# Squares of queries and keys summed in halves and stacked beside the rounded inputs: random features in two matmul passes

## The reference, cut to what matters

```
def _apply_kernel(x, orf):                      # orf: 256 x 64
    proj = einsum('bhld,md->bhlm', x, orf) / d_k ** 0.25
    norm = sum(x * x, axis=-1, keepdims=True) / (2.0 * sqrt(d_k))
    return (exp(proj - norm) + EPS) / sqrt(m)
q_phi, k_phi = _apply_kernel(q, orf), _apply_kernel(k, orf)
kv   = einsum('bhlm,bhld->bhmd', k_phi, v);  ksum = sum(k_phi, axis=2)
num  = einsum('bhlm,bhmd->bhld', q_phi, kv); den = einsum('bhlm,bhm->bhl', q_phi, ksum)
out  = num / den[..., None]
```

## Time and profile before

| | |
|---|---|
| median of 3 runs | 1614.45 us (1612.59 to 1615.34) |
| the profiled execution | 1616.33 us |
| its span | 1614.8 us |
| PE busy (matmul) | 1411.8 us, 87% |
| PEld busy | 1245.2 us, 77% |
| DVE busy | 758.5 us, 47% |
| ACT busy | 465.8 us, 29% |
| POOL busy | 383.8 us, 24% |
| PE's granted clock, mean | 0.949 |

### The profile page before, as it was taken

One profiled execution on the slowest core, in us unless ns is written; L12 is line 12 of the kernel. 1 busy time (PEld: TensorE's weight loads), 2 busy tenths in 40 slices (PEclk: granted clock), 3 DMA queues, 4 the chain that ended last, 5 costly groups with the idle time before them and its releaser, 6 DMA issues.

```text
span 1614.8 us, 26325 instructions
## 1 busy us (share of the span) xinstructions
PE 1411.8 (87%) x8396; PEld 1245.2 (77%) x8460; DVE 758.5 (47%) x1492; ACT 465.8 (29%) x777; POOL 383.8 (24%) x380
## 2 busy tenths in 40 slices
PE   5788878967879999999999999997999499999980
PEld 2566666967879999999999999996888488888860
DVE  7754443414334545444444545345454425444536
ACT  7412222401013333333232424243222113223310
POOL 7422343233221010101010101002224211222233
PEclk9999999988889999999999999999999599999995
DMA  4100111334222020202020202003144326665657
GB/s 150 54 32 23 53 59 56 97 115 123 84 71 85 20 90 14 91 13 91 13 91 13 91 13 78 0 1 120 57 144 139 141 74 237 239 238 215 213 199 279
DMA packets 64532, 158.06 MB, mean 98 GB/s; under 512 B 7978, under 2 KB 28922, under 8 KB 64032
## 3 DMA queue, kind: packets, MB, share of 16 engines
q1 hardware_dynamic: 55200, 127.20, 22.4%
q0 software_dynamic: 9280, 30.17, 6.0%
HBM read 119.98 MB, written 55.71 MB: 109 GB/s over the span
## 4 chain that ended last, share of the span: by engine, by line
PE 76%; DMA 7%; DVE 6%; issue 5%; ACT 2%; POOL 2%; DVEq 1%; SPq 1%; POOLq 0%; ACTq 0%
PE PB L1562 7%; PE PB L1564 7%; PE PB L1563 7%; PE PB L1738 5%; PE PB L1739 5%; PE PB L1741 5%; PE PB L1598 4%; PE PB L1621 4%; PE PB L1466 4%; DMA y_scratch<-xrow 3%; PE PB L1507 2%; PE PB L1544 2%; PE PB L1508 2%; PE PB L1509 2%; PE PB L1545 2%
## 5 line engine op out<-in xcount | busy, mean ns | idle before, releaser
L1562 PE MATMUL PB<-xh,hw 128*128 128x416 f32 (+1 forms) x576 | 206.0, 358 | 7.0 <-POOL orfl L758 7.0
L1564 PE MATMUL PB<-xh,hw 128*128 128x416 f32 (+1 forms) x576 | 204.1, 354 | 0.0
L1563 PE MATMUL PB<-xl,hw 128*128 128x416 f32 (+1 forms) x576 | 203.8, 354 | 0.0
L1738 PE MATMUL PB<-mwh,mth 128*128 128x512 f32 x368 | 149.4, 406 | 1.3 <-issue 1.3
L1466 PE MATMUL PB<-ohs,ohd 128*128 x471 | 107.4, 352 | 46.5 <-DVE ohs L1116 31.6
L1739 PE MATMUL PB<-mwl,mth 128*128 128x512 f32 x368 | 144.7, 393 | 0.0
L703 POOL CAST hw<-hraw 128x1024 fp32r<-128x1024 f32 x24 | 25.1, 1047 | 466.6 <-PE PB L1564 465.8
L1466 PEld LDWEIGHTS PB<-ohs,ohd 128*128 x534 | 52.3, 99 | 100.3 <-issue 82.3
L1562 PEld LDWEIGHTS PB<-xh,hw 128*128 128x128 f32 x576 | 109.4, 190 | 8.4 <-POOL orfl L758 7.2
L1741 PE MATMUL PB<-mwh,mtl 128*128 128x512 f32 x368 | 114.4, 392 | 0.0
L1563 PEld LDWEIGHTS PB<-xl,hw 128*128 128x128 f32 x576 | 109.5, 190 | 1.3
(11 more groups left out here) (260 smaller groups left out, 3135.3 us busy)
## 6 DMA issues: line engine op xcount, KB each, us to landing
mraw<-expert_w SPq DMA_DIRECT2D x64, 512.0 KB, 7.4
slot_y<-x SPq DMA_DIRECT2D x7, 2560.0 KB, 12.2
slot_y<-ybuf SPq DMA_DIRECT2D x46, 256.0 KB, 3.3
count_rests<-ATf POOLq DMA_DIRECT2D x9, 640.0 KB, 3.3
xrow<-x SPq DMA_DIRECT2D x40, 128.0 KB, 2.5
y_scratch<-xrow SPq DMA_DIRECT2D x40, 128.0 KB, 2.4
yrow<-y_scratch SPq DMA_DIRECT2D x20, 256.0 KB, 2.9
x2n_half<-xhat SPq DMA_DIRECT2D x20, 256.0 KB, 2.5
```

The costliest lines, as they stand in the source:

```text
L1562: mm(bank(i, n), hw[:, wi, 0, k, :], xh[:, k, c0:c0 + n], start=(k == 0), stop=False)
L1563: mm(bank(i, n), hw[:, wi, 0, k, :], xl[:, k, c0:c0 + n], start=False, stop=False)
L1564: ins = mm(bank(i, n), hw[:, wi, 1, k, :], xh[:, k, c0:c0 + n], start=False, stop=(k == KT - 1))
L1738: mm(y[c], mth[:, k, :], mwh[par][:, k, c * CW:(c + 1) * CW], start=(k == 0), stop=False)
```

## The change

`sk` becomes `nk`. For each head `nk` holds the rounded inputs in 64 rows and, in the other 64, sums of squares: the squares of rows 0 to 31 and of rows 32 to 63 of a head are added elementwise, so that 32 rows of sums are left; their rounded part takes 32 rows and the rest 32 rows. The stationary block `orfn` holds, per head, the low part of `orf` beside the inputs' rows and -1 beside the sums' rows. A feature then takes two passes: `orfh` with `tk`, `orfn` with `nk`.

ACT gives a chunk its bias, then writes two copies of 64 rows and four squares of 32 rows, and signals `sq_ready` behind the last. DVE casts `qf` into `tk` as before, then waits for `sq_ready`, adds the halves (96 rows), computes the rests of the inputs, casts the sums (twice 32 rows) and computes the sums' rests (twice 32 rows). POOL sets two more buffers, fills 512 columns in place of 256, and subtracts twice in place of once.

```
-        sk = keep("sk", [P, 2, NP], F32R, pb)
+        nk = keep("nk", [P, 2, NP], F32R, pb)
-        qf = keep("qf", [P, CW], F32, pb)
-        sqf = keep("sqf", [P, CW], F32, pb)
+        chunk = keep("chunk", [P, 3, THIRDS[0][1]], F32, pb)
+        qf, sqf, sqg = (chunk[:, i, :] for i in range(3))
-        orfl = keep("orfl", [P, M], F32R, pa)
-        negr = keep("negr", [P, M], F32R, pa)
+        orfn = keep("orfn", [P, 2, M], F32R, pa)
...
-            g.memset(negr[:, :].bitcast(F32), -1.0).then_inc(a_cst, 1)
+            g.memset(orfn[:, :, :].bitcast(F32), -1.0).then_inc(a_cst, 1)
...
-            g.memset(sk[:, :, N:NP].bitcast(F32), 0.0).then_inc(a_cst, 1)
+            g.memset(nk[:, :, N:NP].bitcast(F32), 0.0).then_inc(a_cst, 1)
+            g.memset(sqf[:, :], 0.0).then_inc(a_cst, 1)
+            g.memset(sqg[:, :], 0.0).then_inc(a_cst, 1)
...
-            pool.wait_ge(a_cst, 6)
-            g.tensor_tensor(orfl[:, :], qf[:, 0:M], orfh[:, :].bitcast(F32), ALU.subtract).then_inc(a_cst, 1)
+            pool.wait_ge(a_cst, 8)
+            g.tensor_tensor(orfn[0:64, 0], qf[0:64, 0:M], orfh[0:64, :].bitcast(F32), ALU.subtract).then_inc(a_cst, 1)
+            g.tensor_tensor(orfn[64:128, 1], qf[64:128, 0:M], orfh[64:128, :].bitcast(F32), ALU.subtract).then_inc(a_cst, 1)
+            pool.wait_ge(a_cst, 10)
... ACT, project
-                a.activation(sqf[:, 0:n], qf[:, 0:n], ACT.Square, scale=SQ_SCALE).then_inc(sq_ready, 1)
-                act.wait_ge(sq_ready, START + 6 * j + i + 1)
                 act.wait_ge(phi_done, START + 22 * j + (10 if i >= 3 else 0))
-                a.activation(sk[0:64, 0, c0:c0 + n], sqf[0:64, 0:n], ACT.Copy)
-                a.activation(sk[64:128, 1, c0:c0 + n], sqf[64:128, 0:n], ACT.Copy).then_inc(s_hi, 1)
+                a.activation(nk[0:64, 0, c0:c0 + n], qf[0:64, 0:n], ACT.Copy)
+                a.activation(nk[64:128, 1, c0:c0 + n], qf[64:128, 0:n], ACT.Copy)
+                a.activation(sqf[64:96, 0:n], qf[0:32, 0:n], ACT.Square, scale=SQ_SCALE)
+                a.activation(sqg[64:96, 0:n], qf[32:64, 0:n], ACT.Square, scale=SQ_SCALE)
+                a.activation(sqf[0:32, 0:n], qf[64:96, 0:n], ACT.Square, scale=SQ_SCALE)
+                a.activation(sqg[0:32, 0:n], qf[96:128, 0:n], ACT.Square, scale=SQ_SCALE).then_inc(sq_ready, 1)
... DVE, stack
                 v.tensor_copy(tk[64:128, 1, c0:c0 + n], qf[64:128, 0:n]).then_inc(t_hi, 1)
+                dve.wait_ge(sq_ready, START + 6 * j + i + 1)
+                v.tensor_tensor(sqf[0:96, 0:n], sqf[0:96, 0:n], sqg[0:96, 0:n], ALU.add).then_inc(s_hi, 1)
                 dve.wait_ge(t_hi, 6 * j + i + 1)
...
-                dve.wait_ge(s_hi, 6 * j + i + 1)
-                v.tensor_tensor(sk[64:128, 0, c0:c0 + n], sqf[0:64, 0:n], sk[0:64, 0, c0:c0 + n].bitcast(F32), ALU.subtract)
-                v.tensor_tensor(sk[0:64, 1, c0:c0 + n], sqf[64:128, 0:n], sk[64:128, 1, c0:c0 + n].bitcast(F32),
+                dve.wait_ge(s_hi, 2 * (6 * j + i) + 1)
+                v.tensor_copy(nk[64:96, 0, c0:c0 + n], sqf[64:96, 0:n])
+                v.tensor_copy(nk[0:32, 1, c0:c0 + n], sqf[0:32, 0:n]).then_inc(s_hi, 1)
+                dve.wait_ge(s_hi, 2 * (6 * j + i) + 2)
+                v.tensor_tensor(nk[96:128, 0, c0:c0 + n], sqf[64:96, 0:n], nk[64:96, 0, c0:c0 + n].bitcast(F32), ALU.subtract)
+                v.tensor_tensor(nk[32:64, 1, c0:c0 + n], sqf[0:32, 0:n], nk[0:32, 1, c0:c0 + n].bitcast(F32),
                                 ALU.subtract).then_inc(s_done, 1)
... PE, key_features and query_features
-                        mm(o, tk[:, h, at], orfl[:, :], start=False, stop=False)
-                        ins = mm(o, sk[:, h, at], negr[:, :], start=False, stop=True)
+                        ins = mm(o, nk[:, h, at], orfn[:, h], start=False, stop=True)
...
-                    mm(bank(3 + f % 2, n), orfl[:, m], tk[:, h, c0:c0 + n], start=False, stop=False)
-                    mm(bank(3 + f % 2, n), negr[:, m], sk[:, h, c0:c0 + n], start=False, stop=True).then_inc(phi_done, 1)
+                    mm(bank(3 + f % 2, n), orfn[:, h, m], nk[:, h, c0:c0 + n], start=False, stop=True).then_inc(phi_done, 1)
```

More of the change, by code:

```diff
@@ L941, in high_pass @@
                     high_tile(r, src, p, slice(p * P, (p + 1) * P))
-            act.wait_ge(a_cst, 7)
+            act.wait_ge(a_cst, 10)
             act.wait_ge(s_bias[0], 48)
@@ L1197, in row_pass @@
                     finish(c, t, p, T, TT // 2 - 1)
-            dve.wait_ge(a_cst, 7)
+            dve.wait_ge(a_cst, 10)
             def stack(j, i):
@@ L1547, in row_tile @@
                 ins.then_inc(r.done, 1)
-            pe.wait_ge(a_cst, 7)
+            pe.wait_ge(a_cst, 10)
             def project(j, wi, after=None):
```

## The result

The changed kernel takes 1769.16 us (median of four runs, 1764.77 to 1773.32) against 1613.52 for the kernel before on the same chip: a ratio of 1.0968, 95% interval 1.0931 to 1.1005. The forecast of 1708 had the sign right and was 61 us short; its range ended at 1732. The profiled execution took 1764.77 (span 1763.2), 148.4 more than the one before. PE's mean granted clock went from 0.949 to 0.886. Times and ratios of all kernels are of executions in the fast state (at most 1.5% above the kernel's fastest, the ratio over all of them and not from two medians); the traces of two_buffers and before_wait2 are of slower ones.

A forecast was written before the change was run, and what follows sets the result against it. PE, busy 87% of the span, was taken as the bound, with the single-buffered chunk chain setting the pace after the change. Queries less keys 44.4, turns 24.2, start 1.8 and clock 23 gave 93.4 more: 1708, range 1676 to 1732.

The forecast's parts named there:

- the chunk: ACT and DVE chain: a query chunk is ready 7.88 us after its bias, so biases stand 7.9 us apart.
- the wait for the exponential: Query features: PE waits some 6.7 us for the first query exponential, queued on ACT behind the last chunk.
- at the turn: Turns before the next pair: copy 1 stands behind a longer chunk, so PE waits 3.45 us, in seven pairs.
- the keys: Key features: ten banks lose two of six matmuls, saving 1.15 us per pair.
- POOL's start: Kernel start: PE waits longer for POOL's constants, through a second subtraction and more fills, 1.8 us in all.
- short squares: Rival, chunk chain: squares of 32 partitions take 0.14 us instead of 0.55, giving 1645; chance 0.05.
- overlapping activations: Rival, chunk chain: each of six ACT steps is 0.09 to 0.13 shorter, giving 1689; chance 0.07.
- The step that failed: PE's granted clock halves after idling: 2.0 us per pair at the queries, 1.0 at the turns, 23 in all.
- the key chunks' end covered: Key chunks: three times 7.9 from 706.46 end at 730.2, before PE's values, so no wait arises there.
- Clock kept: Rival, PE's granted clock: the clock term does not occur, 23 less, 1685; chance 0.1.
- More than that: Rival: POOL's split holds a cast of sums and half clock lasts longest, 26 more, 1734; chance 0.08.
- Turns not held: Rival, turns: copy 1 comes early enough, so 31 fall away, 1677; chance 0.06.

The follow-up runs named there:

- two_buffers: The changed kernel with a second buffer for the chunk's inputs and squares, used in turn, so ACT may run one chunk ahead of DVE; 1710.2 us.
- before_wait2: The kernel before, with DVE's four rests of the last query chunk made in ten pieces of 42 columns each; 1641.1 us, ratio 1.0150.
- two_passes_only: The kernel before without the pass of orf's low part in all features, old inputs kept, that product left out; 1590.4 us, ratio 0.9878.
- warm: The changed kernel with spare matmuls of 418 columns filling PE's three waits, results unchanged; 1706.4 us, ratio 1.0563 to the kernel before.
- rewarm: The changed kernel with 16 spare matmuls of 418 columns between query bank 16 and the first outputs, behind the waits; 1744.7 us.
- early: The changed kernel with DVE's rests of the inputs ahead of its wait for `sq_ready` and ACT's squares ahead of its copies; 1718.0 us.
- best: The changed kernel with the edits of two_buffers, early and copy_first together; 1657.0 us, ratio 1.0280 to the kernel before.
- copy_first: The changed kernel with DVE's stack of the next pair's first two chunks behind copies 1 and 3 of the turns; 1775.2 us.
- best_split: best, with POOL splitting the next queries' weights only behind the next pair's key projection; 1599.6 us, ratio 0.9935 to the kernel before.
- best_pool: best, with two of POOL's three weight splits per pair held until the running projection's chunks are finished; 1664.4 us, ratio 1.0338.
- before_wait: The kernel before, with DVE's four rests of the last query chunk made in six pieces of at most 70 columns each; 1617.4 us.

## Why the prediction was wrong

**What held.** The bound, the mechanism and the waits, term by term: the chunk (7.9 forecast, 8.07 and 8.24 measured), the wait for the exponential (6.7 and 6.81), for DVE's rests (2 and 1.77), at the turn (3.45 and 3.45), the keys (-1.15 and -1.19), POOL's start (1.8 forecast; PE's wait grew from 6.95 to 8.7). Squares of 32 rows lasted 0.55, so *short squares* fell, and the copies and squares of a chunk followed one another at 0.56 without overlap, so *overlapping activations* fell too. The 0.09 us of overlap that the Trainium skill ("ScalarE: Activation LUTs", What ACT_TABLE_LOAD costs) gives shows only behind them: the first exponential starts at 733.20, 0.1 ahead of the last square's end. That the passes were on the path is shown by two_passes_only.

**The step that failed is the clock's.** The query features and outputs lost 13.71 us per pair; 6.7 of them are the net waits, so the clock took 7.0, where 2.0 was put down (2.7 as the upper end). warm, with the same waits at the full clock, gives nearly the same split: 6.5 of clock (36.2 - 29.7) and 7.2 of net waits. The turns lost 6.5, of which 3.45 is the wait, so 3.1 in place of 1.0. That is 8 x 5.0 + 7 x 2.1 = 54.7 us.

The profiled execution was 148.4 - 93.4 = 55.0 over the sum, and that the two agree so closely is luck. The first pair lost 6 us more than the others, and PE waited 4.5 us ahead of its key features, where the forecast had the key chunks' end covered. On the other side the kernel outside the attention, which no edit touched, was some 8 us shorter in this execution: from PE's first projection to the end of the last pair's outputs the time went from 641.2 to 795.5 us, 154.3 more, against 148.4 for the whole.

The mis-sizing has a place in the argument. Both rows from which it took "some 3.4 us" and "4.3 us of dense work at half clock" are followed by wide matmuls alone: 418 columns behind 459.84, and 256 columns behind the idle stretch at 163, in the kernel before:

```profile
164.37 0.38 PE L1507 MATMUL PB<-wqh,xh 128*128 128x256 f32 x1 [1.74 <-ACT hrf L916]
```

Behind the wait in the query features stand ten wide matmuls with a second wait between them, and then the outputs of 65 columns, which the forecast counted as dense work of the same kind. At half clock PE spent some 20 us there (733.75 to 753.7), not 4.3. At the turn wide matmuls do follow, and the term failed in another way: it took the shorter of the two rows, 3.4, and discounted it, while the clock fell in each of the seven pairs and was down for 6.8 us, 6.1 of them behind PE's restart, nearer the 5.8 of the other row. warm shows that the clock makes the difference, rewarm that sixteen wide matmuls bring it back where the outputs did not, and before_wait2 that the same wait costs 0, 1 or 7 us of clock. In the changed kernel it was the dear kind in every pair. What the chip goes by in this is not shown by any run.

**The rivals.** *Clock kept* fell with the clock itself. *More than that* (1734) had the right direction for two reasons, and neither in the right size: its longest half clock was again read from projections, and POOL's split cost 0.2 us (8.24 against 8.07), since the cast that it lengthened (1.14 us at 722.09) lay beside ACT's squares and only the addition behind (0.80 in place of 0.59) was on the path. The same split became the last obstacle once the order was mended, and there it took some 2.8 us per chunk (early, best). *Turns not held* was wrong in its price: with the turn freed nothing was gained (copy_first), because the key chunks' own end, counted as covered, was covered only by the wait at the turn; the first pair, which has no turn in front, shows the same in the changed kernel (4.5 us).

**What the runs showed in its place.** The two passes are worth 21 us, and the chunk chain buries them. best_split brings 12 of them home with four edits together: DVE working beside ACT, a second buffer, the turns' copies ahead of the chunks, and POOL's split out of the way. best, which lacks only the last, is 2.8% above the kernel before. Whether the second buffer is needed once the split is out of the way was not tried. Left open are the falls of the clock in the key features of warm and best_split, the shorter low clock in rewarm's turns, and why the clock falls at different points of the same wait.

## What to carry to other kernels

Price an idle stretch of PE by what PE does right behind it: wide matmuls without a wait between them brought the full clock back within some 6 us here, ten microseconds that were mostly outputs of 65 columns did not (739.77 to 749.79), so a wait ahead of narrow matmuls could cost some four times its length (2.03 us of wait, 8.9 in all, in before_wait2). When work moves off PE, lay the helpers' whole chain on the clock (each engine's time per chunk, the buffer's turn-round, and the other engines' long instructions on the same memory) before counting the saved passes. And when a wait is removed, name the one that stood behind it: copy_first, two_buffers and best_pool each took one wait away and met the next.

## What had not been expected of the hardware

PE at 1.2 GHz for some 24 us of a pair (730 to 754) while its busy share was mostly 2.00 of 2.00, and back at 2.4 GHz within 5 us of matmuls of 418 columns (rewarm). An idle stretch of 1.74 us was already followed by a fall (before, at 163), and so was one of 2.03 in six of seven pairs (before_wait2), while one of 0.89 was not in any of seven (before_wait). The same 2.03 us of idleness followed by a fall inside it, by one 0.9 to 1.6 us behind it, or by none. Beside POOL's split DVE's operations of three kinds were lengthened, to about the split's end: a cast of 0.37 to 2.42, a subtraction of 0.59 to 2.65, six epsilons of 1.9 together to 4.79.
